# Fewer candidate products per head in a routing step: 28 in two rectangles instead of an 8 by 8 square

## The chip, the cores and the metric

The kernel runs on one core of a Trainium2 chip. The metric is the device time of one execution in microseconds (us). Engine names are those of the profile: PE is TensorE (PEld its weight loads), DVE is VectorE, ACT is ScalarE, POOL is GpSimd, SP is SyncE.

## The reference, cut to what matters

The program is one transformer layer: linear attention with a feature map, a layer norm, then a feed-forward layer that has a dense gated part and a sparse part of 1024 experts chosen by product keys, and a second layer norm. The input has 8 x 2048 tokens of width 256. The change touches the choice of experts alone:

```python
q = (hidden_states @ Wq).reshape(b, t, 2, H, RET // 2)          # H = 4 heads
sim = jnp.einsum('btphn,hkpn->pbthk', q, keys)                  # 2 x 64 scores per head
sc, ix = jax.lax.top_k(sim, KPH)                                # best 8 of each 64
all_sc = (sx[..., :, None] + sy[..., None, :]).reshape(b, t, H, KPH * KPH)
scores, pk = jax.lax.top_k(all_sc, KPH)                         # best 8 of the 64 sums
...
w = jax.nn.silu(w) * jax.nn.softmax(scores, axis=-1)
```

Both lists of eight are sorted from the largest down. The sum of entry a of one and entry b of the other (counted from 0) has at least (a+1)(b+1) - 1 sums in front of it, so only pairs with (a+1)(b+1) <= 8 can be among the best eight.

## The kernel before, in words

The tokens are worked through in 32 groups of 512, each group as 4 tiles of 128 rows (t = 0 to 3). The work is a software pipeline: in one iteration, group a has its keys and values summed (bank `kv_bank`), a group four behind has its attention computed (`at_bank`), the group after that has its experts chosen ("routing", `rt_bank`), the next its feed-forward product (`ring`, `pt_bank`, `y_bank`), and the last its second norm and its store. Every engine has its own list of instructions, written out by hand per iteration as eight steps c = 0 to 7; engines meet at semaphores only, and an engine's list is worked off in order. A routing tile t takes the two steps c = 2t and 2t + 1.

One routing tile runs like this:

- PE forms the 2 x 4 x 64 scores of 128 tokens in `rt_bank`. On DVE, `scores(t)` takes the best eight of each 64 (`top`, L913), writes all scores less the largest into the tile `ex` (L916), and the best eight less the largest behind them (L918). `ex` is `[128, 8, 64 + 8]`: rows 0 to 3 belong to the first half of the key of the four heads, rows 4 to 7 to the second half.
- ACT takes the exponential of the whole of `ex` in place (L744) and signals `rt_exp`. Two engines wait for that signal, DVE with `choose(t)` and POOL with `spread(t, 0)`.
- On DVE, `choose(t)` multiplies the eight exponentials of one half by the eight of the other, 64 products per head, into `cand` (L924), takes the best eight of the 64 for each of the four heads (`best`, L929), sums them (`zsum`, L932) and inverts the sum (`rz`, L934).
- On POOL, `spread(t, h)` forms for head h the full grid of 16 x 64 = 1024 products of the exponentials into `grid` (L390). There are two buffers, so heads 0 and 1 go ahead at once, and heads 2 and 3 wait until DVE has used up the buffer. It reads only the first 16 values of the first half (1024 experts over 64 keys).
- On DVE, `keep(t, h)` sets to zero what is below the eighth best (L940) and `add_head(t, h)` adds the head, over its sum, to `prob` (L952 for h = 0, L955 for the others). `keep(t, 0)` waits for the grid of head 0 and stands behind `choose(t)` in DVE's list.

Between these, DVE's list has pieces of the other groups: the low parts of the queries and keys (`qT_hl`, `kT_hl`, L820), the attention quotient (`den`, L882 and L884, then `x`, L886), the two norms (L868, L871, L906, L994), the running sum `kv_sum` (L841), the gate (L971) and the expert weights (`wexp`, L977). POOL's list has, beside the grids, small additions to `kp` (L359) and `qp` (L381), the bias of `xb` (L376) and two tiny steps per norm (L367, L369). In each iteration PE's `kv_bank` product (L518) needs `kp` from POOL, and its L553 and L480 products need the low parts from DVE.

Which values of `ex` are read after the exponential is what the change rests on: `spread` reads columns 0 to 15 of rows 0 to 3 and columns 0 to 63 of rows 4 to 7, and `choose` reads columns 64 to 71 of all rows. Columns 16 to 63 of rows 0 to 3 are computed and then read by nothing.

Of the kernel before, what the change touches and what calls it, by code (L numbers as in the profile page):

```python
# [23 lines left out]
ALU = mybir.AluOpType  # L24
# [3 lines left out]
P = 128  # L28


def block_kernel(nc, x, Wq, bq, Wk, bk, Wv, bv, Wo, bo, rw, Wg, bg, Wu, bu, Wd, bd,
# [10 lines left out]
    RH, NK, _, RN = keys.shape  # L42
    TOP = 8
    NX = NEXP // NK
# [26 lines left out]
    with ExitStack() as ctx:  # L71
        def sb(name, *shape, dt=F32):
            return ctx.enter_context(nc.sbuf_tensor(name, list(shape), dt))
# [39 lines left out]

        top = sb("top", P, 2 * RH, TOP)
        ex = sb("ex", P, 2 * RH, NK + TOP)
        cand = sb("cand", P, RH, TOP, TOP)
        best = sb("best", P, RH, TOP)
        zsum, rz = sb("zsum", P, RH), sb("rz", P, RH)
        grid = sb("grid", P, 2, NX, NK)
# [142 lines left out]
        def bcast(ap, shape):  # L262
            return ap.broadcast_to(shape)
# [524 lines left out]
        def _(dve):  # L788
# [69 lines left out]
            def body(it, par, kv, at, rt, ff, last, batch):  # L858
                a, m, s, n, f = it, it - ATTN_LAG, it - ROUTE_LAG, it - FFN_LAG, it - LAST_LAG
# [61 lines left out]
                def choose(t):  # L921

                    dve.wait_ge(rt_exp, s * T + t + 1)
                    rt_steps.mark(dve.tensor_tensor(  # L924
                        cand[:], bcast(ex[:, 0:RH, NK:].unsqueeze(3), [P, RH, TOP, TOP]),
                        bcast(ex[:, RH:, NK:].unsqueeze(2), [P, RH, TOP, TOP]), ALU.mult))
                    rt_steps.wait_apart()
                    for h in range(RH):
                        ins = dve.max(best[:, h, :], cand[:, h].rearrange("p a b -> p (a b)"))  # L929
                    rt_steps.mark(ins)  # L930
                    rt_steps.wait()
                    rt_steps.mark(dve.reduce_sum(zsum[:], best[:], AX.X))  # L932
                    rt_steps.wait()
                    marks["rz"] = rt_steps.mark(dve.reciprocal(rz[:], zsum[:]))  # L934
# [69 lines left out]
                for c in range(C):  # L1004
# [33 lines left out]
                    if rt and not odd and c:  # L1038
                        choose(t)
# [3 lines left out]
                    if rt and c == 0:  # L1043
                        choose(0)
# [47 lines left out]
```

## Time and profile before

| | |
|---|---|
| median of 3 runs | 4222.05 us (4220.74 to 4226.71) |
| profiled execution, first to last instruction (its span) | 4221.7 us |
| time of the profiled execution beside its span | none is listed; the span lies 0.35 us under the median |
| PE busy | 3856.7 us, 91% of the span |
| DVE busy | 3091.4 us, 73% |
| POOL busy | 1802.3 us, 43% |
| ACT busy | 1340.1 us, 32% |
| chain that ended last, by engine | PE 68%, issue 11%, DVE 10%, POOL 8%, ACT 3% |

How to read it: busy times are sums over all instructions of an engine, and a share of 91% on PE says only that PE is rarely idle. The chain that ended last is followed back from the last instruction to whatever released each step; its shares tell on which engine the time went that could not have been saved elsewhere. In the views by line, each instruction has its start and duration in us from the start of the span, and in square brackets how long its engine sat idle before it and what ended that.

### The profile page before, as it was taken

To read this page: it belongs to the slowest core of one execution; us is meant where nothing else is said; L and a number is where in the kernel's file an instruction comes from. 1 tells how busy PE (TensorE), PEld (TensorE's weight loads), DVE (VectorE), ACT (ScalarE), POOL (GpSimd) and SP (SyncE) were. 2 spreads that over 40 slices of the span, in tenths; PEclk is the share of its full clock that TensorE was granted. 3 is DMA by queue.
4 is the path that set the end of the run, shared out by engine and by line. 5 is a ranking of instruction groups with operands and counts; after the bars stand their busy time and mean duration, and the time that the engine had idled before them with its cause. 6 is when DMAs were issued, how large, how long until landed. Compare 5 with 4: busy or idle time off the path is not lost.

```text
span 4221.7 us, 58223 instructions
## 1 busy us (share of the span) xinstructions
PE 3856.7 (91%) x19260; PEld 3189.8 (76%) x19260; DVE 3091.4 (73%) x5938; ACT 1340.1 (32%) x1926; POOL 1802.3 (43%) x1100
## 2 busy tenths in 40 slices
PE   8868999999999999999899999999999999998988
PEld 6757777787777787777787777787777787777777
DVE  2277787777777777778777777777878677887884
ACT  3223333323333323333323333323333323333321
POOL 1144444444444444544444444444444444444441
PEclk8769999999999999999999999999999999999999
DMA  3000000000000000000000000000000000000000
GB/s 101 11 10 6 16 16 16 11 11 16 11 16 16 11 11 16 11 16 16 11 11 16 11 16 16 11 11 16 11 16 16 11 11 6 11 11 11 11 6 11
DMA packets 23384, 61.74 MB, mean 15 GB/s; under 512 B 5552, under 2 KB 10032, under 8 KB 23088
## 3 DMA queue, kind: packets, MB, share of 16 engines
q1 hardware_dynamic: 18480, 41.04, 3.0%
q0 software_dynamic: 4608, 16.78, 1.0%
q8 instruction: 183, 3.00, 0.3%
q14 instruction: 113, 0.93, 0.1%
HBM read 41.04 MB, written 16.78 MB: 14 GB/s over the span
## 4 chain that ended last, share of the span: by engine, by line
PE 68%; issue 11%; DVE 10%; POOL 8%; ACT 3%; POOLq 0%; DVEq 0%; SPq 0%; ACTq 0%; DMA 0%
PE ring L539 18%; PE y_bank L623 8%; PE y_bank L625 8%; PE at_bank L562 6%; PE kv_bank L518 5%; POOL grid L390 5%; PE rt_bank L539 4%; DVE grid L940 3%; PE at_bank L488 3%; POOL kp L359 3%; PE kv_bank L488 3%; PE at_bank L474 2%; PE at_bank L553 2%; PE kv_bank L480 2%; PE at_bank L480 2%
## 5 line engine op out<-in xcount | busy, mean ns | idle before, releaser
L390 POOL TENSOR_TENSOR grid<-ex 128x1024 f32<-128x1024 f32 x512 | 1214.1, 2378 | 527.4 <-DVE prob L952 239.8
L940 DVE SCALAR_TENSOR_TENSOR grid<-grid,best 128x1024 f32<-128x1024 f32 x512 | 784.1, 1531 | 87.8 <-POOL grid L390 86.6
L955 DVE SCALAR_TENSOR_TENSOR prob<-grid,rz,prob 128x1024 f32<-128x1024 f32 x384 | 651.3, 1696 | 12.6 <-DVE grid L940 5.7
L623 PE MATMUL y_bank<-wd_sb,gate 128*128 128x256 f32 x2048 | 647.9, 399 | 5.2 <-DVE wexp L977 5.2
L625 PE MATMUL y_bank<-up_sb,wexp 128*128 128x256 f32 x2048 | 633.8, 392 | 0.0
L381 POOL TENSOR_SCALAR qp<-qp 128x512 f32<-128x512 f32 x256 | 224.5, 877 | 694.2 <-ACT qp L735 687.6
L539 PE MATMUL ring<-x1T_hl,wg_hl 128*128 128x512 f32 x1536 | 450.9, 431 | 42.6 <-issue 40.4
L625 PEld LDWEIGHTS y_bank<-up_sb,wexp 128*128 128x128 f32 x2048 | 404.7, 198 | 59.8
L539 PE MATMUL ring<-x1T_hl,downT_hl 128*128 128x512 f32 x1536 | 426.6, 413 | 21.2 <-ACT gate L749 21.2
L539 PE MATMUL ring<-x1T_hl,wu_hl 128*128 128x512 f32 x1536 | 439.5, 423 | 0.0
L623 PEld LDWEIGHTS y_bank<-wd_sb,gate 128*128 128x128 f32 x2048 | 369.7, 199 | 51.4 <-issue 19.5
L539 PEld LDWEIGHTS ring<-x1T_hl,wg_hl 128*128 128x128 f32 x1536 | 291.7, 200 | 115.0 <-issue 57.6
L359 POOL TENSOR_SCALAR kp<-kp 128x1024 f32<-128x1024 f32 x120 | 177.3, 1477 | 440.7 <-ACT kp L716 433.9
L749 ACT ACTIVATE gate<-ring,bg_sb 128x512 f32<-128x512 f32 x256 | 176.4, 689 | 589.4 <-PE ring L539 587.9
L539 PEld LDWEIGHTS ring<-x1T_hl,wu_hl 128*128 128x128 f32 x1536 | 299.4, 198 | 77.9 <-issue 14.3
L518 PEld LDWEIGHTS kv_bank<-v_sb,kp 128*128 128x128 f32 x1920 | 256.6, 212 | 126.2 <-POOL kp L359 86.6
L518 PE MATMUL kv_bank<-v_sb,kp 128*128 128x33 f32 x1920 | 260.2, 294 | 97.9 <-POOL kp L359 97.9
L539 PEld LDWEIGHTS ring<-x1T_hl,downT_hl 128*128 128x128 f32 x1536 | 276.7, 189 | 95.7 <-ACT gate L749 32.1
L754 ACT ACTIVATE wexp<-ring 128x512 f32<-128x512 f32 x256 | 153.3, 599 | 493.6 <-PE ring L539 493.0
L562 PEld LDWEIGHTS at_bank<-kv_blocks,qp 128*128 128x128 f32 x2048 | 277.7, 211 | 12.6 <-DVE x L886 2.3
L376 POOL TENSOR_TENSOR xb<-xb,bo_sb 128x1024 f32<-128x1024 f32 x32 | 75.5, 2360 | 494.8 <-PE at_bank L474 494.8
L971 DVE SCALAR_TENSOR_TENSOR gate<-ring,bu_sb,gate 128x512 f32<-128x512 f32 x256 | 191.1, 746 | 108.8 <-PE ring L539 106.9
(117 smaller groups left out, 5631.8 us busy)
## 6 DMA issues: line engine op xcount, KB each, us to landing
xb<-in_L_attn_x SPq DMA_DIRECT2D x34, 512.0 KB, 3.4
out_y<-x POOLq DMA_DIRECT2D x32, 512.0 KB, 3.0
xa<-in_L_attn_x SPq DMA_DIRECT2D x30, 512.0 KB, 3.4
prob<-in_L_ffn_down_embed SPq DMA_DIRECT2D x1, 1024.0 KB, 6.1
prob<-in_L_ffn_Wg SPq DMA_DIRECT2D x1, 1024.0 KB, 8.9
prob<-in_L_ffn_Wu SPq DMA_DIRECT2D x1, 1024.0 KB, 10.5
wd_sb<-in_L_ffn_Wd SPq DMA_DIRECT2D x1, 1024.0 KB, 11.7
up_sb<-in_L_ffn_up_embed SPq DMA_DIRECT2D x1, 1024.0 KB, 11.9
```

Of the source, the lines that this page charges most:

```text
L359: pool.tensor_scalar(lane.kp[:], lane.kp[:], ATTN_EPS, 1.0, ALU.add, ALU.mult).then_inc(lane.eps, 1)
L381: pool.tensor_scalar(qp[:, j % 4], qp[:, j % 4], ATTN_EPS, 1.0, ALU.add, ALU.mult).then_inc(qp_eps, 1)
L390: pool.tensor_tensor(grid[:, h % 2], bcast(ex[:, h, 0:NX].unsqueeze(2), [P, NX, NK]), bcast(ex[:, RH + h, 0:NK].unsqueeze(1), [P, NX, NK]) ...
L488: mm = pe.matmul(bank[:, (t - t0) * D:(t - t0 + 1) * D], srcT[:, k, t * P:(t + 1) * P], w[:, k, :], start=(k == 0), stop=(k == KD - 1))
L518: mm = pe.matmul(bank[:, c * VW:(c + 1) * VW], lane.kp[:, c * P:(c + 1) * P], lane.v[:, j % 2, c, :], start=True, stop=True)
L539: mm = pe.matmul(bank[:], st if swap else wt, wt if swap else st, start=(k == 0 and i == 0), stop=(k == KD - 1 and i == 2))
L562: mm = pe.matmul(at_bank[:, (2 * t + c) * W:(2 * t + c + 1) * W], qp[:, (2 * j + c) % 4, t * P:(t + 1) * P], kv_blocks[:, 2 * j + c].rearr ...
L623: pe.matmul(rows, gate[:, c % 2, t * P:(t + 1) * P], wd_sb[:, c, :], start=(c == 0 and t % 2 == 0), stop=False, skip_group_check=True)
L625: mm = pe.matmul(rows, wexp[:, c % 2, t * P:(t + 1) * P], up_sb[:, c, :], start=False, stop=(c == C - 1), skip_group_check=True)
L940: marks["keep", h] = rt_steps.mark(dve.scalar_tensor_tensor(out=g, in0=g, scalar=best[:, h, TOP - 1:TOP], in1=g, op0=ALU.is_ge, op1=ALU.mult))
L955: ins = dve.scalar_tensor_tensor(out=row, in0=g, scalar=rz[:, h:h + 1], in1=row, op0=ALU.mult, op1=ALU.add, accum_out=mass[:, 0:1] if h == ...
L971: dve.scalar_tensor_tensor(out=gate[:, c % 2], in0=ring[1 - c % 2][:], scalar=bu_sb[:, c:c + 1], in1=gate[:, c % 2], op0=ALU.add, op1=ALU. ...
```

## The change

`choose(t)` forms 28 of the 64 products per head instead of all: the eight of the first half by the best two of the second (16), and the best two of the first half by the other six of the second (12). That takes two multiplications one behind the other on DVE where there was one of 256 elements; the first has 64 elements per partition, the second 48. Only the first waits for `rt_exp`, only the second signals. The four maxima read 28 values each instead of 64. The tile `cand` is gone: its name stands now for columns 16 to 43 of rows 0 to 3 of `ex`. No other engine's list changes, and no wait is added or taken away.

```diff
-        cand = sb("cand", P, RH, TOP, TOP)
+        cand = ex[:, 0:RH, NX:NX + 2 * TOP + 2 * (TOP - 2)]
...
                     dve.wait_ge(rt_exp, s * T + t + 1)
+                    xs8, ys8 = ex[:, 0:RH, NK:], ex[:, RH:, NK:]
+                    dve.tensor_tensor(
+                        cand[:, :, 0:2 * TOP].rearrange("p h (a b) -> p h a b", b=2),
+                        bcast(xs8.unsqueeze(3), [P, RH, TOP, 2]),
+                        bcast(ys8[:, :, 0:2].unsqueeze(2), [P, RH, TOP, 2]), ALU.mult)
                     rt_steps.mark(dve.tensor_tensor(
-                        cand[:], bcast(ex[:, 0:RH, NK:].unsqueeze(3), [P, RH, TOP, TOP]),
-                        bcast(ex[:, RH:, NK:].unsqueeze(2), [P, RH, TOP, TOP]), ALU.mult))
+                        cand[:, :, 2 * TOP:].rearrange("p h (a b) -> p h a b", a=2),
+                        bcast(xs8[:, :, 0:2].unsqueeze(3), [P, RH, 2, TOP - 2]),
+                        bcast(ys8[:, :, 2:].unsqueeze(2), [P, RH, 2, TOP - 2]), ALU.mult))
                     rt_steps.wait_apart()
                     for h in range(RH):
-                        ins = dve.max(best[:, h, :], cand[:, h].rearrange("p a b -> p (a b)"))
+                        ins = dve.max(best[:, h, :], cand[:, h])
```

## Rows read from the trace of the kernel before

**Rows 1.** The page, part 1: busy us (share of the span) and instructions of each engine.
```profile
PE 3856.7 (91%) x19260; PEld 3189.8 (76%) x19260; DVE 3091.4 (73%) x5938; ACT 1340.1 (32%) x1926; POOL 1802.3 (43%) x1100
```
**Rows 2.** Waits of PE: waiting line <- releaser: us in total, times, longest us.
```profile
PE kv_bank L518 <- POOL kp L359: 97.9, 65, 9.8
PE at_bank L553 <- DVE qT_hl L820: 54.4, 32, 4.2
```
**Rows 3.** DVE by line: busy us, mean ns | idle before us <- releaser.
```profile
L924 DVE TENSOR_TENSOR cand<-ex 128x256 f32<-128x256 f32 x128 | 100.3, 784 | 84.6 <-ACT ex L744 84.6
```
**Rows 4.** Instructions of lines L924 and L918: duration ns min/median/max.
```profile
L924 DVE TENSOR_TENSOR cand<-ex x128: 412/425/2126, 234.6 to 4126.3; 128x256 f32<-128x256 f32 x128
...
L918 DVE TENSOR_TENSOR ex<-top x128: 212/216/2403, 230.7 to 4124.0; 128x64 f32<-128x64 f32 x128
```
**Rows 5.** Timeline of DVE, first tile of an iteration: start us, us, instruction [idle before].
```profile
1466.29 0.41 DVE L924 TENSOR_TENSOR cand<-ex 128x256 f32<-128x256 f32 x1
...
1468.50 2.91 DVE L940 SCALAR_TENSOR_TENSOR grid<-grid,best 128x1024 f32<-128x1024 f32 x1 [0.66 <-POOL grid L390]
```
**Rows 6.** Timeline of POOL, the same tile: grids of heads 0 and 1.
```profile
1466.27 2.19 POOL L390 TENSOR_TENSOR grid<-ex 128x1024 f32<-128x1024 f32 x1 [2.42 <-ACT ex L744]
...
1468.43 1.90 POOL L390 TENSOR_TENSOR grid<-ex 128x1024 f32<-128x1024 f32 x1
```
**Rows 7.** Timeline of PE behind that tile.
```profile
1473.01 0.73 PE L553 MATMUL at_bank<-qT_hl,rw_hl 128*128 128x512 f32 x2 [1.51 <-DVE qT_hl L820]
...
1477.32 1.13 PE L480 MATMUL kv_bank<-xaT,wk_sb 128*128 128x512 f32 x2 [1.41 <-DVE kT_hl L820]
```
**Rows 8.** Timeline of DVE, second tile of the same iteration.
```profile
1492.40 0.43 DVE L924 TENSOR_TENSOR cand<-ex 128x256 f32<-128x256 f32 x1 [1.09 <-ACT ex L744]
...
1495.83 0.17 DVE L882 TENSOR_SCALAR den<-at_bank 128x16 f32<-128x16 f32 x1 [1.86 <-PE at_bank L562]
```
**Rows 9.** Timeline of POOL, second tile: grid of head 0.
```profile
1492.53 2.06 POOL L390 TENSOR_TENSOR grid<-ex 128x1024 f32<-128x1024 f32 x1 [1.39 <-ACT ex L744]
```
**Rows 10.** Timeline of DVE, fourth tile of the same iteration.
```profile
1554.75 2.06 DVE L924 TENSOR_TENSOR cand<-ex 128x256 f32<-128x256 f32 x1
...
1557.88 1.78 DVE L940 SCALAR_TENSOR_TENSOR grid<-grid,best 128x1024 f32<-128x1024 f32 x1
...
1560.44 1.28 DVE L940 SCALAR_TENSOR_TENSOR grid<-grid,best 128x1024 f32<-128x1024 f32 x1
...
1562.30 2.26 DVE L955 SCALAR_TENSOR_TENSOR prob<-grid,rz,prob 128x1024 f32<-128x1024 f32 x1
1564.48 2.05 DVE L940 SCALAR_TENSOR_TENSOR grid<-grid,best 128x1024 f32<-128x1024 f32 x1
```
**Rows 11.** Timeline of POOL, fourth tile: grids of heads 0, 1 and 2, then kp.
```profile
1554.64 1.89 POOL L390 TENSOR_TENSOR grid<-ex 128x1024 f32<-128x1024 f32 x1
...
1556.50 2.08 POOL L390 TENSOR_TENSOR grid<-ex 128x1024 f32<-128x1024 f32 x1
1560.60 2.87 POOL L390 TENSOR_TENSOR grid<-ex 128x1024 f32<-128x1024 f32 x1 [2.02 <-DVE prob L952]
1563.56 1.90 POOL L359 TENSOR_SCALAR kp<-kp 128x1024 f32<-128x1024 f32 x1
```
**Rows 12.** Timeline of PE behind the fourth tile.
```profile
1565.52 0.74 PE L518 MATMUL kv_bank<-v_sb,kp 128*128 128x33 f32 x5 [0.61 <-POOL kp L359]
```
**Rows 13.** Timeline of DVE in an earlier iteration: L918 and the next instruction.
```profile
1340.04 2.40 DVE L918 TENSOR_TENSOR ex<-top 128x64 f32<-128x64 f32 x1
1342.37 0.68 DVE L977 TENSOR_TENSOR wexp<-pt_bank,wexp 128x512 f32<-128x512 f32 x1
```
**Rows 14.** Timeline of POOL at the same place.
```profile
1339.99 2.37 POOL L376 TENSOR_TENSOR xb<-xb,bo_sb 128x1024 f32<-128x1024 f32 x1 [17.89 <-PE at_bank L474]
```
**Rows 15.** Two stretches: us, busy us of PE, PEld, DVE, ACT, POOL, granted clock, DMA share, GB/s.
```profile
1500.00:1520.00 20.00, 17.81 (x92) 15.04 (x91) 11.92 (x25) 3.52 (x7) 9.66 (x6) 0.91 0.00 1
...
1464.00:1480.00 16.00, 12.15 (x43) 7.52 (x43) 14.90 (x24) 8.53 (x12) 8.88 (x5) 1.00 0.01 1
```

## Prediction, made before the changed kernel was run

> **What bounds the kernel now.** I read the page first: PE is busy for 91% of the span [rows 1], so an edit on DVE can only be worth what PE waits for DVE or for something behind DVE. The table of PE's waits comes next. Two entries can hear of this change: PE waits 54.4 us, 32 times, for the low part of the queries from DVE, and 97.9 us for `kp` from POOL [rows 2]. Then the table by line: the product takes 784 ns in the mean over 128 tiles [rows 3]. The reader should see that this mean hides two cases: the median is 425 ns and the longest 2126 ns [rows 4]. The sum shows how often: 100.3 - 128 x 0.425 = 45.9 us too much, and at 2.06 instead of 0.425 us apiece [rows 10] that is 28 tiles.
>
> The timelines of DVE and POOL side by side tell what happens in those 28. In the fourth tile POOL starts the grid of head 0 at 1554.64 and takes 1.89 us; DVE's product starts at 1554.75 and ends 0.28 us after the grid, at 1556.81 [rows 10, 11]. In the first tile the two start 0.02 us apart; now the product takes 0.41 us and the grid 2.19, where the grid behind it takes 1.90 [rows 5, 6]. Both read two operands from SBUF, and one of them stands still while the other runs. A third case is two such DVE instructions one behind the other with POOL waiting: L955 runs from 1562.30 to 1564.56, `kp` on POOL starts at 1563.56 and ends at 1565.46, and L940 behind L955 takes 2.05 us instead of 1.28 [rows 10, 11]. POOL, waiting already, goes in **between** the two. The change replaces one product by such a pair, so the question at each tile is whether POOL's grid falls between them.
>
> **The change, part by part.** Prices first. A product of 64 elements is 0.216 us by L918 [rows 4]. From 64 to 256 elements the median grows by 209 ns, 1.09 ns an element, so that 48 elements give some 0.20 us. The instruction behind L918 starts 0.07 us before L918 ends [rows 13]; I take 0.08. The pair, if nothing comes between, then takes 0.13 + 0.20 = 0.33 us instead of 0.425. No row shows a maximum over 28 values; it lies between no gain and 36 x 1.09 = 39 ns saved. I take the slope, four times, 0.16 us a tile. The freed SBUF and the writes into `ex` I cost at nothing: the columns written are read by no other engine, and DVE, which overwrites them with the next tile's scores, stands behind the maxima in its own list. In all DVE has 0.26 us a tile less to do, 33 us over 128 tiles, most of which is waiting time regained as waiting time. By tile:
>
> *Second and third tile.* DVE has its maxima, sum and inverse done, then waits 1.86 us for PE [rows 8]. That covers a gain. It would also cover a loss: were the second product held until the grid is over, `choose` would end about 1495.5, still before 1495.83. Here the grid starts 0.13 us after the product [rows 8, 9], the pair is most likely through. Worth nothing either way.
>
> *First tile.* POOL's grid asks at the same time as the product and gets its turn 0.29 us late (2.19 against 1.90) [rows 5, 6]. With a first product of 64 elements it waits 0.21 us less, and, as it is waiting by then, I expect it to go between the two products. The second product then ends about 0.05 us after the grid, at 1468.30, and the chain of maxima, sum and inverse (0.10 + 0.48 + 0.44) makes `keep` ready at 1469.3. This costs nothing: `keep` is held until the grid of head 1 ends, 1470.33 now [rows 5, 6] and 1470.12 then. So `keep` ends 0.21 us earlier, and with it the low parts of queries and keys for which PE waits 1.51 and 1.41 us [rows 7]. The two waits are in series behind the same DVE list, so 0.21 counts once: 32 x 0.21 = 6.7 us. If the pair stays together here, it is 0.10 and 3.2 us.
>
> *Fourth tile.* The first product gets its turn when the grid of head 0 ends at 1556.53, and itself ends 0.07 us later (a 0.425 one ends 0.28 later). The second starts 0.08 before that, at about 1556.52. The grid of head 1 starts at 1556.50 [rows 11]. This is the knife's edge. In the first tile POOL's start was 0.02 us the earlier, and DVE won [rows 5, 6]; over an L918 [rows 13, 14] it was 0.05 us the earlier, and DVE lost (2.40 us for L918). The pair here is at the first of these two, and DVE has the operands' path in hand already, so I take it that the pair stays together. Then the grid of head 1 is held for 0.33 instead of 0.425 us, `keep`, held by it, ends 0.10 earlier, and so do L952, the grid of head 2, `kp`, and PE's wait of 0.61 us [rows 10 to 12]: 28 x 0.10 = 2.8 us.
>
> Sum: 6.7 + 2.8 = 9.5 us less than the span of 4221.7 us, which lies 0.35 us under the median; from the median, **4212.6 us**. That is 0.22%, at the edge of what a measurement of this kernel can tell from no change (some 0.2%, 8.4 us).
>
> The pair rests on a second instruction that starts before the first has ended, as L977 does behind L918 [rows 13]. The Trainium skill, "VectorE: DVE Perf Modes", section "The DRAIN you can't avoid", speaks against the change: an operation starts only when the pipe of the one before it is empty, so few operations are better than short ones. This trace doesn't agree as far as recorded starts go (0.07 us of overlap); by that rule the second product would start at 1556.60, after POOL, and the sum would be that of the first rival.
>
> **Rivals.** *POOL goes between the pair in the fourth tile (slower).* The second product is held until the grid of head 1 ends, about 1556.50 + 1.89 = 1558.39, and ends at 1558.44. From the product's end to `keep`'s start it was 1.07 us [rows 10]; less 0.16 that gives 1559.35, and with 1.28 us for a free `keep` its end is 1560.63 instead of 1559.66, 0.97 later. L952, the grid of head 2 and `kp` follow one upon the other [rows 10, 11], and PE, now waiting 0.61, waits 1.58 us [rows 12]. 28 x 0.97 = 27.2, less the first tile's 6.7: +20.5, 4242.5 us. It decides when the second product's start falls more than some 0.02 to 0.05 us behind POOL's, so a first product that is only slightly slower than L918 brings it about. For it: every recorded pair with POOL waiting was split. Against it: in those POOL came well before the first had ended.
>
> *The same, and the clock falls.* In the stretch with the iteration's other, longer wait of PE for `kp` the granted clock is 0.91 over 20 us [rows 15], which is 3.6 us at the lower of the two levels, some 1.8 us lost. If a wait of 1.58 us did this too, 28 x 1.8 = 50 us would come on top: 4293 us. Against it: the stretch with waits of 1.51 and 1.41 us [rows 7] has the full clock, 1.00 [rows 15].
>
> *Hidden.* PE's waits in the first tile shrink, but what PE then meets comes no earlier, since it hangs on ACT or on POOL's other work; the time stays at 4219 to 4224 us. For it: the whole edit is small against the waits of 1 to 2 us around it.
>
> **How the numbers follow.** Forecast 0.52, pair split in the fourth tile 0.34, split with the clock 0.05, hidden 0.09. The forecast's own range is 4206 to 4219 (first tile 0.10 or 0.21, maxima with or without gain, some drift); two thirds of it lie beyond 0.2%. So faster by over 0.2% 0.35 (0.34 of the forecast, 0.01 of hidden), within 0.2% 0.27 (0.18, 0.08 and 0.01 of the split), slower 0.38 (0.33 and 0.05). The range takes in the forecast and the split with some drift and leaves out the clock: 4206 to 4250.
>
> **What would show it.** Right: in the fourth tile the two products run one behind the other in about 0.33 us after the grid of head 0, PE's wait for `kp` there is near 0.51 us, and the wait for the query part in the first tile near 1.30. Wrong: the second product takes near 1.9 us in the fourth tile and PE waits near 1.6 us for `kp`. The forecast also falls if POOL's first-tile grid still takes 2.1 us or more, or if PE's waits shrink as said and the span doesn't.

## The result, and the profile after

| | before | after |
|---|---|---|
| median of runs on the same chip | 4224.16 us (4220.74 to 4226.71, 4 runs) | 4290.15 us (4288.67 to 4295.76, 4 runs) |
| ratio | | 1.017 (95% interval 1.0152 to 1.0189) |
| span of the profiled execution | 4221.7 us | 4294.1 us |

The change made the kernel 1.7% slower. The forecast was 4212.6 us, the range ended at 4250; what came is the second rival, for which 4293 us had been worked out and to which 1 chance in 20 had been given.

The page after, part 1, answers to [rows 1]. DVE is as busy as before (3091.4 us then), though `choose` now multiplies less than half as many values:

```profile
PE 3902.1 (91%) x19260; PEld 3228.6 (75%) x19260; DVE 3099.2 (72%) x6066; ACT 1339.4 (31%) x1926; POOL 1792.8 (42%) x1100
```

PE's waits after (waiting line <- releaser: us in total, times, longest) answer to [rows 2]; lines have moved by two. The wait for `kp` has grown from 97.9 to 123.8 us, that for the low part of the queries has shrunk from 54.4 to 52.5:

```profile
PE kv_bank L520 <- POOL kp L361: 123.8, 65, 8.8
PE at_bank L555 <- DVE qT_hl L822: 52.5, 32, 3.8
```

DVE by line after (busy us, mean ns | idle before) answers to [rows 3]:

```profile
L931 DVE TENSOR_TENSOR ex<-ex 128x48 f32<-128x48 f32 x128 | 89.3, 698 | 0.0
L927 DVE TENSOR_TENSOR ex<-ex 128x64 f32<-128x64 f32 x128 | 73.0, 570 | 85.3 <-ACT ex L746 85.2
L937 DVE MAX8 best<-ex 128x8 f32<-128x28 f32 x512 | 58.5, 177 | 13.2
```

The maxima gained what the slope said (177 ns each; it said 214 - 39 = 175). The two products together are busy for 162.3 us, where the one took 100.3. The reader should look for why a product of 48 values takes 698 ns in the mean, and the timelines of the fourth tile show it. DVE:

```profile
1587.44 1.86 DVE L927 TENSOR_TENSOR ex<-ex 128x64 f32<-128x64 f32 x1
1589.22 1.92 DVE L931 TENSOR_TENSOR ex<-ex 128x48 f32<-128x48 f32 x1
1591.25 0.46 DVE L937 MAX8 best<-ex 128x8 f32<-128x28 f32 x4
...
1592.06 1.28 DVE L948 SCALAR_TENSOR_TENSOR grid<-grid,best 128x1024 f32<-128x1024 f32 x1
```

and POOL at the same place, the grids of heads 0, 1 and 2 and `kp` (against [rows 11]):

```profile
1587.32 1.89 POOL L392 TENSOR_TENSOR grid<-ex 128x1024 f32<-128x1024 f32 x1
...
1589.18 1.90 POOL L392 TENSOR_TENSOR grid<-ex 128x1024 f32<-128x1024 f32 x1
1594.29 2.87 POOL L392 TENSOR_TENSOR grid<-ex 128x1024 f32<-128x1024 f32 x1 [3.21 <-DVE prob L960]
1597.24 1.90 POOL L361 TENSOR_SCALAR kp<-kp 128x1024 f32<-128x1024 f32 x1
```

The first product is held by the grid of head 0, as before. The second is held by the grid of head 1, which now runs unhindered (1.90 us, 2.08 before): as recorded it starts 0.12 us before the first product ends, and ends 0.06 us before the second does. `keep` ends 5.90 us after the product began, 4.91 before [rows 10]. The second product is held in this way in 27 of the 32 fourth tiles. PE waits 1.61 us for `kp` where it waited 0.61 [rows 12]:

```profile
1599.20 0.97 PE L520 MATMUL kv_bank<-v_sb,kp 128*128 128x33 f32 x7 [1.61 <-POOL kp L361]
```

Behind that wait the granted clock falls. One stretch around this fourth tile, after (us, busy us of PE, PEld, DVE, ACT, POOL, granted clock, DMA share, GB/s):

```profile
1588.00:1608.00 20.00, 18.13 (x97) 15.48 (x97) 17.61 (x22) 3.91 (x6) 10.61 (x5) 0.91 0.00 1
```

and the same stretch of the kernel before:

```profile
1555.00:1575.00 20.00, 18.65 (x108) 15.93 (x106) 17.62 (x22) 4.70 (x7) 11.11 (x5) 1.00 0.00 1
```

One iteration proves little, because in both kernels the clock alternates between two levels (0.5 and 1.00 of full speed, 1.2 and 2.4 GHz) all along. So a stretch of 10 us, beginning 1 us before this wait ends (to the nearest us), was read in all 26 iterations after the first that have the wait (0.61 us before and 1.61 after in 24 of them, 0.6 us longer in two). Before, the clock is below 1.00 in 2 of the 26 and its mean is 0.98. After, it is below 1.00 in 25 of the 26 and its mean is 0.79. That is 49 us of full-speed time not granted (26 x 10 us x 0.19).

Over the whole span the mean granted clock went from 0.940 to 0.930. A clock of 0.930 over 4294.1 us is 301 us of full-speed time not granted, 0.940 over 4221.7 us is 253: 48 us more. As far as these digits go, the whole of it is lost at this one place. With the 25.9 us of waiting for `kp` that is 74 us, against 72.4 us between the two spans. (The clock is given to three digits, so each of the two products is good to some 2 us each way.)

### The profile page after: what moved, and what is told of

It reads as the page before. It is cut to its first block and busy times, and to the rows that moved or that the text cites. A ratio compares the mean times of both kernels' runs of the same rounds, so it can differ in the third digit from the quotient of the medians.

```text
span 4294.1 us, 58351 instructions
## 1 busy us (share of the span) xinstructions
PE 3902.1 (91%) x19260; PEld 3228.6 (75%) x19260; DVE 3099.2 (72%) x6066; ACT 1339.4 (31%) x1926; POOL 1792.8 (42%) x1100
## 5 line engine op out<-in xcount | busy, mean ns | idle before, releaser
L392 POOL TENSOR_TENSOR grid<-ex 128x1024 f32<-128x1024 f32 x512 | 1201.7, 2354 | 566.4 <-DVE prob L960 274.4
L948 DVE SCALAR_TENSOR_TENSOR grid<-grid,best 128x1024 f32<-128x1024 f32 x512 | 766.7, 1497 | 81.8 <-POOL grid L392 81.0
L625 PE MATMUL y_bank<-wd_sb,gate 128*128 128x256 f32 x2048 | 667.9, 410 | 6.7 <-DVE wexp L985 6.7
L627 PE MATMUL y_bank<-up_sb,wexp 128*128 128x256 f32 x2048 | 645.9, 399 | 0.0
L627 PEld LDWEIGHTS y_bank<-up_sb,wexp 128*128 128x128 f32 x2048 | 416.3, 203 | 64.8
L625 PEld LDWEIGHTS y_bank<-wd_sb,gate 128*128 128x128 f32 x2048 | 379.1, 204 | 53.5 <-issue 21.0
L520 PE MATMUL kv_bank<-v_sb,kp 128*128 128x33 f32 x1920 | 280.6, 307 | 123.8 <-POOL kp L361 123.8
L520 PEld LDWEIGHTS kv_bank<-v_sb,kp 128*128 128x128 f32 x1920 | 276.7, 226 | 152.0 <-POOL kp L361 110.6
L564 PEld LDWEIGHTS at_bank<-kv_blocks,qp 128*128 128x128 f32 x2048 | 268.6, 205 | 11.9 <-DVE x L888 2.3
L718 ACT ACTIVATE kp<-kv_bank 128x512 f32<-128x512 f32 x240 | 143.4, 598 | 397.7 <-PE kv_bank L514 396.3
```

Of the source, the lines that this page charges most:

```text
L392: pool.tensor_tensor(grid[:, h % 2], bcast(ex[:, h, 0:NX].unsqueeze(2), [P, NX, NK]), bcast(ex[:, RH + h, 0:NK].unsqueeze(1), [P, NX, NK]) ...
L520: mm = pe.matmul(bank[:, c * VW:(c + 1) * VW], lane.kp[:, c * P:(c + 1) * P], lane.v[:, j % 2, c, :], start=True, stop=True)
L564: mm = pe.matmul(at_bank[:, (2 * t + c) * W:(2 * t + c + 1) * W], qp[:, (2 * j + c) % 4, t * P:(t + 1) * P], kv_blocks[:, 2 * j + c].rearr ...
L625: pe.matmul(rows, gate[:, c % 2, t * P:(t + 1) * P], wd_sb[:, c, :], start=(c == 0 and t % 2 == 0), stop=False, skip_group_check=True)
L627: mm = pe.matmul(rows, wexp[:, c % 2, t * P:(t + 1) * P], up_sb[:, c, :], start=False, stop=(c == C - 1), skip_group_check=True)
L948: marks["keep", h] = rt_steps.mark(dve.scalar_tensor_tensor(out=g, in0=g, scalar=best[:, h, TOP - 1:TOP], in1=g, op0=ALU.is_ge, op1=ALU.mult))
```

## The experiments

The theory after the result: in the fourth tile POOL's grid of head 1 goes between the two products; that delays `kp` and makes PE wait 1.0 us longer in each of 26 iterations; and behind the longer wait the clock is at its lower level for longer. On the chip of these runs (all but the one with the long fill) the kernel before itself varies more (4203 to 4255 us over all its runs there), so ratios with their intervals are compared. Each run below was timed against the kernel before on its own chip.

**Which tile.** The pair in the fourth tile alone:

```diff
+        cand64 = sb("cand64", P, RH, TOP, TOP)
...
+                    if t == T - 1:
                         (the two products)
+                    else:
+                        (the one product of 64, into cand64)
```

> The pair of products in the fourth tile of each group alone; the other three tiles keep the one product of 64 in a tile of its own. Split theory (in the fourth tile POOL's grid of head 1 goes between the two products, PE waits 1.0 us more for kp, and the granted clock is low for longer behind that wait): all of the loss stays, 4286 to 4297 us, the second product takes 1.9 us in 26 tiles. Rival by number of instructions (each pair costs, in whatever tile): about a quarter of the loss, near 4240 us. Rival by place (products written into the tile that POOL reads): also about a quarter, near 4240 us.

Measured: 4291.64 us, ratio 1.015 (1.0087 to 1.0213). PE's waits for `kp` sum to 124.1 us, and the second product is held in 27 of the 32 fourth tiles. Within this interval, all of the loss is there.

The reverse has the condition `t != T - 1`.

> The reverse: the pair in the first three tiles, one product of 64 in a tile of its own in the fourth. Split theory: the loss is gone and the first tile's 0.1 us an iteration remains as a gain, 4215 to 4225 us; PE's waits for kp sum to 97 to 98 us as before. Rival by number or by place: three quarters of the loss, near 4272 us.

Measured: 4221.75 us, ratio 0.9986 (0.9961 to 1.0011), PE's waits for `kp` 99.2 us. The loss is gone. The small gain of the first tile can't be told from none. Three pairs out of four cost nothing, so neither the number of instructions nor their place makes the loss.

**The place of the products.** They are written into a tile of their own:

```diff
-        cand = ex[:, 0:RH, NX:NX + 2 * TOP + 2 * (TOP - 2)]
+        cand = sb("cand", P, RH, 2 * TOP + 2 * (TOP - 2))
```

> The changed kernel with the 28 products in a tile of their own instead of the dead columns. Split theory: no difference from the changed kernel, 4286 to 4297 us. Rival by place: back to about 4220 us.

Measured: 4308.44 us, ratio 1.0184 (1.013 to 1.0238), waits for `kp` 124.7 us. The time lies above the 4286 to 4297 us expected, but the ratio agrees with the changed kernel's (1.0152 to 1.0189): that the products are written into the tile that POOL reads has no part in the loss.

**PE's wait and the clock, without any pair.** The kernel before, with a needless sum that delays `keep` in the fourth tile (values of its output are not used):

```diff
+        extra = sb("extra", P, 1)
...
                     rt_steps.mark(ins)
+                    if t == T - 1:
+                        dve.reduce_sum(extra[:], wd_sb[:].rearrange("p c d -> p (c d)")[:, 0:1340], AX.X)
```

> The kernel before with one needless sum over 1340 values behind the maxima of the fourth tile, about 1.47 us on DVE that takes nothing from POOL: 0.5 us of it lie in the time for which DVE is held by the grid of head 1 anyway, so keep for head 0 ends some 0.95 us later, as in the changed kernel, with no pair at all. Split theory with the clock: near the changed kernel, 4280 to 4300 us, PE's waits for kp sum to 120 to 126 us and the clock is at the lower level for some 100 us more than before. Rival (the clock's loss in the changed kernel is an accident that goes with other timings, and only PE's wait counts): 25 to 27 us over the kernel before, near 4250 us.

Measured: 4273.07 us, ratio 1.0103 (1.0071 to 1.0135), +45 us between the medians; waits for `kp` 120.2 us. PE's wait behind the fourth tile:

```profile
1586.38 1.97 PE L519 MATMUL kv_bank<-v_sb,kp 128*128 128x33 f32 x16 [1.46 <-POOL kp L360]
```

In the 10 us around the end of this wait the clock is below 1.00 in 25 of 26 iterations, with a mean of 0.79: the same as in the changed kernel, and 49 us more not granted there than before. So a longer wait of PE at this place is enough for the clock's loss at this place; neither the pair nor other accidents of the change are needed for it.

Over the whole span less is lost. The profiled execution has a clock of 0.935 over 4268.6 us, 277 us not granted, only 24 more than before (some 50 us at the lower level, where 100 were expected); with 22.3 us more waiting that is 46 of the 46.9 us by which its span is longer. The rest of the span thus gave back some 25 us, and no run shows why. For this reason, and because the delay was a little smaller than meant (22.3 us instead of 25.9), the time is below the 4280 expected, but it is twice what the wait alone gives.

The same with 880 values:

> The kernel before with a needless sum over 880 values behind the maxima of the fourth tile, about 1.0 us on DVE, of which 0.5 us lie in a time for which DVE is held anyway: keep for head 0 some 0.47 us later, PE's wait for kp there 1.05 us instead of 0.61. If the clock's loss grows with the wait: half of what the full delay cost, 20 to 25 us over the kernel before. If the clock falls only behind a wait as long as 1.4 to 1.6 us: PE's wait alone, 12 to 14 us.

Measured: 4224.78 us, ratio 1.001 (0.9986 to 1.0034); waits for `kp` 106.1 us, 8.2 us more than before. PE's wait behind the fourth tile:

```profile
1574.17 1.97 PE L519 MATMUL kv_bank<-v_sb,kp 128*128 128x33 f32 x16 [0.97 <-POOL kp L360]
```

The 20 to 25 us of the one expected case did not come: the medians are the same. The interval (6 us less to 14 us more) leaves room for the wait alone. At the place itself the clock did suffer: in the 10 us around the end of the wait it is below 1.00 in 10 of 26 iterations, mean 0.91, some 19 us more not granted than before. But over the whole span the clock is 0.946, which is 26 us less not granted than before, so the rest of the span gave back some 45 us, 22 of them in the 11 us that follow. At this place, then, the clock's fall becomes more frequent with the wait: 2 of 26 iterations at 0.61 us, 10 at 0.97, 25 at 1.46 and at 1.61. What that costs in the whole depends on the rest of the span too.

**What decides who goes first.** The forecast had compared the recorded starts of the second product and of POOL's grid. One run, with 36 products per head, made the first product smaller and so brought the second forward (against the kernel before):

```diff
...
+                    dve.tensor_tensor(cand[:, :, 0:TOP], xs8, bcast(ys8[:, :, 0:1], [P, RH, TOP]), ALU.mult)
                     rt_steps.mark(dve.tensor_tensor(
...
+                        cand[:, :, TOP:].rearrange("p h (a b) -> p h a b", a=4),
+                        bcast(xs8[:, :, 0:4].unsqueeze(3), [P, RH, 4, TOP - 1]),
+                        bcast(ys8[:, :, 1:].unsqueeze(2), [P, RH, 4, TOP - 1]), ALU.mult))
```

> The pair cut otherwise: first the eight of one half by the best of the other (32 elements), then the best four by the other seven (112 elements), 36 products per head in the dead columns, in all tiles. The first product is 32 elements shorter, so the second starts some 0.03 us sooner: in the fourth tile 0.007 us behind POOL's start of the grid of head 1 instead of 0.040. Split theory with the order of asking as what decides: a start 0.013 us behind still went first in the second and third tile, so now the pair stays together in the fourth too: PE's waits for kp near 96 us, time 0.0 to 0.4% under the kernel before. Rival (POOL, standing waiting behind a held instruction, always goes between a pair): as slow as the changed kernel, 1.5 to 1.9% over.

Measured: 4267.16 us, ratio 1.0105 (1.007 to 1.0139), waits for `kp` 127.5 us. The expectation fell: the pair was split. The rival's time (1.5 to 1.9% over) didn't come either, although the waits are the longest of all runs. The clock lost 44 us more than before in the 10 us around this wait (24 of 26 iterations, mean 0.81), but only some 11 us more over the whole span. Its fourth tile on DVE:

```profile
1586.21 1.83 DVE L927 TENSOR_TENSOR ex<-ex 128x32 f32<-128x32 f32 x1
1587.96 2.02 DVE L928 TENSOR_TENSOR ex<-ex 128x112 f32<-128x112 f32 x1
```

and POOL's grid of head 1:

```profile
1587.96 1.90 POOL L392 TENSOR_TENSOR grid<-ex 128x1024 f32<-128x1024 f32 x1
```

Both starts are recorded at 1587.96, and POOL went first. In four first tiles of the same run, too, the grid of head 1 followed directly on the grid of head 0 behind a held first product, and in three of them the order was the other way round: in one, the grid's start is recorded at 474.09 and the second product's at 474.10, and the product went first (0.26 us, the grid 2.03).

The other run moved POOL back, with a fill between the two grids of the fourth tile:

```diff
+        pause = sb("pause", P, 4)
...
                     if rt and not odd:
+                        if t == T - 1:
+                            pool.memset(pause[:], 0.0)
                         spread(t, 1)
```

> The changed kernel with a needless fill of 4 values on POOL between the grids of head 0 and head 1 in the fourth tile, so that POOL asks for the second grid some 0.1 us later. Split theory: the second product of the fourth tile comes first, PE's waits for kp fall back to 98 to 103 us and the time to within 0.3% of the kernel before. Rival (any pair in the fourth tile is held, whoever asks first): 1.5 to 1.9% over the kernel before.

Measured: 4316.17 us, ratio 1.0235 (1.0202 to 1.0269), waits for `kp` 125.0 us. This fell too, and the loss is above the rival's 1.5 to 1.9%: the fill took 0.09 us, moved POOL's start to 1588.40 in the iteration looked at, the second product started at 1588.40 as well, and was held for 1.97 us. That was so in 25 fourth tiles; in one, with the same two starts, the product went first. So the fill was too short to settle the order. The third run has a fill of 192 values:

> As before with a longer pause: a needless fill of 192 values on POOL between the grids of head 0 and head 1 in the fourth tile, some 0.25 us, so that POOL's start of the second grid is recorded 0.15 to 0.2 us behind that of the second product. With the fill of 4 values it was recorded 0.002 us behind and POOL still went first. Split theory: the second product now goes first and takes about 0.2 us; the grid of head 1 ends 0.15 us later than in the kernel before, PE's waits for kp sum to 100 to 104 us, and the time is within 0.5% of the kernel before. Rival (something else in the fourth tile holds the second product or makes the loss): 1.5 to 2.4% over the kernel before, as in the runs with the pair split.

Measured: 4227.6 us, ratio 1.0011 (0.9985 to 1.0037), waits for `kp` 98.2 us. DVE in its fourth tile:

```profile
1576.69 1.86 DVE L930 TENSOR_TENSOR ex<-ex 128x64 f32<-128x64 f32 x1
1578.48 0.20 DVE L934 TENSOR_TENSOR ex<-ex 128x48 f32<-128x48 f32 x1
```

and POOL:

```profile
1578.42 0.25 POOL L426 MEMSET pause<- 128x192 f32 x1
1578.64 1.90 POOL L393 TENSOR_TENSOR grid<-ex 128x1024 f32<-128x1024 f32 x1
```

With POOL busy for 0.25 us at something needless, the second product takes 0.20 us instead of 1.92 in all but one of the fourth tiles, and the whole loss of 1.7% is gone. The clock is back as well: below 1.00 in 3 of 26 iterations around the wait, mean 0.96. This is the plainest proof of the theory: the pair is in all four tiles, as in the changed kernel, and beside the fill only the order of two instructions differs.

**A version that beats both.** The eight exponentials of a half are sorted, and the largest less itself is 0, so the products with the other half's best are the eight themselves, which lie in columns 64 to 71 of `ex`. One product of 4 by 7 right in front of them completes the candidates; this rests on an exponential of 0 that is exactly 1:

```diff
+        cand = ex[:, 0:RH, NK - 4 * (TOP - 1):]
...
                     rt_steps.mark(dve.tensor_tensor(
...
+                        cand[:, :, 0:4 * (TOP - 1)].rearrange("p h (a b) -> p h a b", a=4),
+                        bcast(ex[:, 0:RH, NK:NK + 4].unsqueeze(3), [P, RH, 4, TOP - 1]),
+                        bcast(ex[:, RH:, NK + 1:].unsqueeze(2), [P, RH, 4, TOP - 1]), ALU.mult))
```

> One product again, of the best four of the first half by the seven of the second behind its best (112 elements), written right in front of the eight of the first half, which are themselves the products with the best of the second (its exponential is that of 0). The maxima read 36 values. There is no second product that could be held, and POOL waits 0.15 us less than before in the first and in the fourth tile: 32 x 0.15 + 28 x 0.15 = 9 us under the kernel before, 0.998 of it (0.996 to 1.000).

Measured: 4205.35 us, ratio 0.9957 (0.9937 to 0.9977), 18.8 us between the medians. Waits for `kp` fell to 92.9 us and those for the query part to 49.7: 9.7 us together, the 9 of the expectation. The time fell by more than that, just beyond the expected range (0.996 to 1.000). How much of it is the shorter waits and how much the clock isn't shown: the profiled execution, with a clock of 0.948, is the fastest of the twelve, and over all runs the median clock is 0.945 against 0.940, which alone would be some 22 us. In the first tile POOL's grid is held for 0.14 us instead of 0.29 (2.04 us; 2.19 in [rows 6]):

```profile
1456.15 2.04 POOL L392 TENSOR_TENSOR grid<-ex 128x1024 f32<-128x1024 f32 x1 [2.43 <-ACT ex L746]
```

## Why the prediction was wrong, by its own steps

*Prices: right.* The first product unhindered takes 0.22 us, the second starts 0.14 us behind it and takes 0.20 (0.13 and 0.20 said); the maxima take 0.46 us together where they took 0.61.

*Second and third tile: right in what they are worth*, as the run without a pair in the fourth tile shows. The second product was held in 4 and in 3 of the 32 iterations, and that cost nothing.

*First tile: the step failed, harmlessly.* I expected POOL's grid between the two products and a gain of 0.21 us an iteration. The pair stayed together. DVE:

```profile
1497.46 0.22 DVE L927 TENSOR_TENSOR ex<-ex 128x64 f32<-128x64 f32 x1
1497.60 0.20 DVE L931 TENSOR_TENSOR ex<-ex 128x48 f32<-128x48 f32 x1
```

POOL, starting 0.01 us before the first product and held for 0.21 us:

```profile
1497.45 2.11 POOL L392 TENSOR_TENSOR grid<-ex 128x1024 f32<-128x1024 f32 x1 [2.41 <-ACT ex L746]
```

PE's wait there became 1.43 us, from 1.51 [rows 7]: the 0.10 of the other case, nearly. Over the run these waits fell by 1.9 us, where 3.2 was said for that case.

*Fourth tile: the step that made the forecast wrong.* "I take it that the pair stays together" rested on recorded starts 0.02 us apart, read off two other places at which the order had gone once this way and once that. The second product started 0.04 us behind POOL and was held. The runs show that nearness of recorded starts was the wrong thing to argue from: with 0.00 us between them, in two kernels, POOL also went first, and in the first tile DVE went first with POOL's start 0.15 us ahead of the second product's. What was right is the price of the rival: `keep` 0.99 us later (0.97 said), PE's wait 1.61 us (1.58 said). The 28 held products of the prediction's sum were 26 fourth tiles and 2 first ones, a small slip.

The prediction took from the Trainium skill ("VectorE: DVE Perf Modes", section "The DRAIN you can't avoid") that an operation starts only when the pipe is empty. It left out that the same section goes on: "A next op that is not held starts earlier". As far as recorded starts go the trace agrees with that second sentence (0.14 us from start to start, 0.22 us for the first product). The sum that the prediction tied to the rule, the first rival's, was nearer to the result than the forecast, but by POOL's turn and not by this rule.

*The clock: mis-sized chance.* 1.8 us a time and 50 us in all were said and some 48 were measured. I held it unlikely because the stretch with waits of 1.51 and 1.41 us runs at full clock [rows 15]. That another place with waits as long keeps its clock was no evidence for this one. The runs show that here the clock falls in 2 of 26 iterations behind a wait of 0.61 us and in 25 behind waits of 1.46 and 1.61 us. That the price came out so close is partly luck: it was read from a single stretch elsewhere, and in the other runs with the pair split in the fourth tile the same mechanism gave 4267 to 4316 us.

The range was wrong by the same choice: it left this case out as the last 1 in 20, while it was the likely end of a case to which I gave 0.34.

## What to carry to other kernels

Splitting one short instruction of DVE that reads two operands from SBUF into two can give POOL a place to go between them, and then the second costs not its own 0.2 us but a whole POOL instruction (1.9 us here). Before counting elements saved, look in the trace for the tiles where the instruction is held already: there the split can be held twice, and who goes first can't be settled from recorded starts a few hundredths apart; a form that stays one instruction avoids the question. And where PE has just below a microsecond of idle time in front of it, price a further microsecond at the wait plus the time at the lower clock behind it: 1.5 to 2.2 us more at this place, of which the rest of the span gave back nothing in the changed kernel and more than all in the run with the half delay.

## What the runs showed of the hardware that was not expected

- Recorded starts don't tell whether POOL goes between a DVE pair. In the changed kernel's fourth tiles it did in 27 of 32 cases, in 26 of them as a grid that followed directly on another, recorded 0.04 to 0.05 us ahead of the second product. In the other 96 tiles it did in 10. Where POOL came out of a wait, it went between with its start 0.09 to 0.10 us ahead, but not with 0.01 us (second and third tile) or with 0.13 us and more (first tile). And a grid that followed directly on another came second in three first tiles of the run with the smaller first product. Whether an instruction asks earlier than its recorded start, or the turn passes to the other engine in some order, these runs don't tell: in the run with the long fill POOL's grid was not asking yet.
- The Trainium skill ("SBUF — State Buffer", section "Who interferes with whom") has it that a DVE instruction with two SBUF inputs contends with a GpSimd instruction that reads SBUF, and that the order of issue decides which of them blocks. The blocking agrees (1.92 us for 48 values that take 0.20 us alone). The order of issue can't be read from recorded starts, as the first tile shows.
- At one and the same place the granted clock fell the more often the longer PE had waited: in 2 of 26 iterations behind 0.61 us, in 10 behind 0.97 us, in 25 behind 1.46 us. What the whole span lost by it varied: 48 us in the changed kernel, 24 with the full delay, 26 less than before with the half.
